# Cross attention with sparsemax and a nine-expert feed-forward: another order of the pipeline's pieces, one value product for both row tiles, and round signals and buffers doubled by parity

## The reference

```
q  = LN(x) @ Wq + bq;  k = ctx @ Wk + bk;  v = ctx @ Wv + bv      # 16 heads of 16
s  = (q . k) / 4                                                  # 256 x 16 heads x 77
a  = sparsemax(s)                                                 # max(s - tau, 0), tau so that it sums to 1
x1 = x + (a . v) @ Wo + bo
z  = LN(x1);  l = z @ gate_w.T
two experts of eight are chosen by l + lb_bias; their weights are sigmoid(l), divided by their sum
y  = x1 + sum over experts e of weight_e * (relu(z @ w1_e.T)^2 @ w2_e.T)
        + relu(z @ cfc.T)^2 @ cproj.T                             # the shared expert
```

## Time and profile before

| | |
|---|---|
| executions | 870.45, 864.1, 865.37 us; median 865.37 |
| span of the profiled execution | 863.6 us |
| PE busy | 768.4 us, 89% of the span |
| DVE busy | 606.6 us, 70% |
| POOL busy | 518.4 us, 60% |
| ACT busy | 461.1 us, 53% |
| DMA moved | 34.88 MB |

### The profile page before, as it was taken

The page is one execution under the profiler, slowest core; times in us unless marked ns, Lnnn a source line. Parts: engine busy times, 40 slices in busy tenths (PEclk is TensorE's granted clock), DMA queues, the critical chain, the costliest instruction groups (busy, mean ns, idle before and its releaser), DMA issues.

```text
span 863.6 us, 15088 instructions
## 1 busy us (share of the span) xinstructions
PE 768.4 (89%) x5056; PEld 628.9 (73%) x5056; DVE 606.6 (70%) x1827; ACT 461.1 (53%) x794; POOL 518.4 (60%) x590
## 2 busy tenths in 40 slices
PE   1666449999999899999999999999999999899998
PEld 1544337877878787878788787877787888688877
DVE  1788977878687878777786877887877778742221
ACT  1545454656655566656566566656665656442321
POOL 2459585758666675757586766667575757541010
PEclk9958668999999999999999999999999999999999
DMA  8300001020202002020102020110202020202010
GB/s 254 124 7 14 8 12 51 13 66 5 75 1 74 9 14 62 13 68 16 62 5 74 6 74 2 50 32 14 62 13 68 3 62 2 61 2 62 2 62 12
DMA packets 37358, 34.88 MB, mean 40 GB/s; under 512 B 23153, under 2 KB 34078, under 8 KB 35230
## 3 DMA queue, kind: packets, MB, share of 16 engines
q1 hardware_dynamic: 34934, 28.88, 11.9%
q0 software_dynamic: 1248, 4.73, 1.6%
q10 hardware_dynamic: 1096, 0.29, 0.2%
HBM read 28.30 MB, written 4.33 MB: 38 GB/s over the span
## 4 chain that ended last, share of the span: by engine, by line
PE 41%; DVE 23%; POOL 11%; DMA 11%; issue 8%; ACT 3%; DVEq 1%; ACTq 0%; POOLq 0%
PE y_ps L816 14%; PE h_ps L803 11%; DVE fsum L947 8%; DMA sw_all<-sw_scratch 8%; POOL over L342 7%; PE m_ps L767 6%; PE s_ps L759 4%; PE m_ps L776 4%; DVE g L1092 3%; DVE fold_a L959 2%; ACT hid L577 2%; DMA sw_scratch<-swT 2%; DVE den L967 1%; DVE f_stats L895 1%; DVE ln_stats L895 1%
## 5 line engine op out<-in xcount | busy, mean ns | idle before, releaser
L342 POOL TENSOR_TENSOR over<-S,tau 128x1232 f32<-128x1232 f32 x128 | 286.5, 2249 | 201.3 <-DVE tau L977 198.8
L816 PE MATMUL y_ps<-w_sb,hid 128*128 128x256 f32 x1152 | 279.1, 385 | 23.0 <-ACT hid L577 22.9
L803 PE MATMUL h_ps<-x1nT,w_sb 128*128 128x256 f32 x1152 | 275.6, 382 | 0.0
L816 PEld LDWEIGHTS y_ps<-w_sb,hid 128*128 128x128 f32 x1152 | 211.6, 190 | 65.5 <-ACT hid L577 37.5
L803 PEld LDWEIGHTS h_ps<-x1nT,w_sb 128*128 128x128 f32 x1152 | 215.1, 191 | 30.5 <-issue 2.8
L577 ACT ACTIVATE hid<-g 128x512 f32<-128x512 f32 x144 | 89.9, 625 | 113.3 <-DVE g L1092 112.8
L947 DVE TENSOR_REDUCE fsum<-over 128x16 f32<-128x1232 f32 x96 | 137.0, 1427 | 16.2 <-POOL over L342 13.8
L1092 DVE SCALAR_TENSOR_TENSOR g<-h_ps,sw_all 128x512 f32<-128x512 f32 x128 | 87.5, 684 | 75.1 <-PE h_ps L803 43.0
L526 ACT ACTIVATE signs<-over 128x1232 bf16<-128x1232 f32 x96 | 115.1, 1225 | 22.9 <-POOL over L342 22.9
L923 DVE MAX8 top<-S 128x8 f32<-128x77 f32 x512 | 74.6, 223 | 3.3 <-ACT S L516 3.3
L342 POOL TENSOR_TENSOR attn<-S,tau 128x1232 f32<-128x1232 f32 x32 | 71.8, 2263 | 6.1 <-PE s_ps L759 5.8
(11 more groups left out here) (111 smaller groups left out, 941.9 us busy)
## 6 DMA issues: line engine op xcount, KB each, us to landing
sw_all<-sw_scratch SPq DMA_DIRECT2D x16, 1024.0 KB, 5.3
x_sb<-in_x SPq DMA_DIRECT2D x16, 256.0 KB, 2.7
w_sb<-in_w POOLq DMA_DIRECT2D x2, 2048.0 KB, 12.0
out_y<-wk_sb SPq DMA_DIRECT2D x16, 256.0 KB, 5.7
sw_all<-in_ctx SPq DMA_DIRECT2D x1, 1078.0 KB
v_block<-v_all SPq DMA_DIRECT2D x56, 9.6 KB
wk_sb<-in_wk SPq DMA_DIRECT2D x1, 256.0 KB
wv_sb<-in_wv SPq DMA_DIRECT2D x1, 256.0 KB
```

Of the source, the lines that this page charges most:

```text
L342: return pool.tensor_tensor(dst, S[:, p, t, :, 0:NK], tau[:, p, t].rearrange("p (h o) -> p h o", o=1).broadcast_to([P, NH, NK]), ALU.subtract)
L803: last = pe.matmul(h_ps[:, i % 2, c, :], w1_sb[:, e, k, c * P:(c + 1) * P], x1nT[:, p, k, :], start=(k == 0), stop=(k == KC - 1))
L816: last = pe.matmul(y_ps[:, t, :], hid[:, i % 2, c, t * P:(t + 1) * P], w2_sb[:, e, c, :], start=(i == 0 and t == 0 and c == 0), stop=(i == ...
```

## The change

1. New order. `turns` now runs b = -1 to 18. The pieces are called one by one in a new order on every engine. The feed-forward part of batch f begins in turn f+2 (layer1 0 to 7, layer2 0 to 4) and ends in turn f+3 (layer2 5 to 8, layer1 8). The attention product of batch m is in PE's turn m+1 instead of m+2, and so are output, second norm and route. `newton` is cut into `round_sum`, `round_lean`, `round_fold`, `round_count`, `round_step`, `last_sum`, `last_step`. The count of unsettled rows moves from y_ps to a bank of s_ps.
2. Joint value product. `attnT` holds both tiles. Both tiles' attention is turned first, with layer1(4) between, then `late_heads` multiplies once: 17 blocks with 256 rows moving; one ACT copy of 512 numbers per partition to OT, then `late_output` for both tiles.
3. A signal for each load: eight semaphores in the place of `w_att`, each waited for where its data is used first. The feed-forward weights are issued by SP. The start values are raised half by POOL, half by PE.
4. Signals and small buffers of the rounds (`fold_a`, `fold_b`, `lean`, `fsum`, `rden`, `step`) are doubled by the batch's parity.

The core of the diff:

```diff
-        attnT = sb("attnT", [P, CHUNKS, P])
+        attnT = sb("attnT", [P, CHUNKS, TOK])
-        tau_first, tau_ready = sig("tau_first", T), sig("tau_ready", ROUNDS)
+        tau_first, tau_ready = sig2("tau_first", T), sig2("tau_ready", ROUNDS)
...
-            for b in range(NB + 3):
-                turn(b, b % 2, 1 - b % 2, new=b < NB, mid=1 <= b < NB + 1, late=2 <= b < NB + 2, old=b >= 3,
-                     ahead=b < NB - 1)
+            for b in range(-1, NB + 3):
+                turn(b, b % 2, 1 - b % 2, ahead=b < NB - 1, new=0 <= b < NB, mid=0 <= b - 1 < NB, late=0 <= b - 2 < NB,
+                     old=b >= 3)
...
-            for s in signals:
-                pool.sem_inc(s.sem, s.per)
+            for s in signals[0::2]:
+                pool.sem_inc(s.sem, s.per)
...
+            for s in signals[1::2]:
+                pe.sem_inc(s.sem, s.per)
             pe.wait_ge(consts, N_CONSTS)
+            pe.wait_ge(ident_loaded, 16)
...
+            def late_heads(m):
                 pe.wait_ge(v_placed[m // 2 % 2], 16 * len(PIECES) * (m // RING + 1))
+                pe.wait_ge(gate_chain.sem, gate_chain.at(m - 1, 1))
                 for i, blocks in enumerate(BY_BANK):
-                    pe.wait_ge(aT_taken.sem, aT_taken.at(m, SB * t + i + 1))
+                    pe.wait_ge(aT_taken.sem, aT_taken.at(m, SB + i + 1))
                     for c, a in blocks:
-                        last = pe.matmul(m_ps[32 * quad:32 * quad + 32, t, half * P:(half + 1) * P],
+                        last = pe.matmul(m_ps[32 * quad:32 * quad + 32, 0, half * TOK:(half + 1) * TOK],
                                          v_block[0:rows, m % RING, BLOCKS.index((c, a)), :], attnT[0:rows, c, :],
                                          start=c == order[0], stop=c == order[-1])
...
+            def late_heads(m):
+                act.wait_ge(o_done.sem, o_done.at(m))
                 act.wait_ge(wo_done.sem, wo_done.at(m - 1))
-                act.activation(OT[:, :, t * P:(t + 1) * P], pair(t), ACT.Copy).then_inc(o_taken.sem, 1)
+                act.activation(OT[:].rearrange("p k n -> p (k n)"), m_ps[:, 0, :], ACT.Copy).then_inc(o_taken.sem, 1)
...
-    nc = bacc.Bacc("TRN2", target_bir_lowering=False, num_devices=1)
+    nc = bacc.Bacc("TRN2", target_bir_lowering=False, num_devices=1, dynamic_dma_scratch_size=1024)
```

More of the change, by code:

```diff
@@ L83, in sig, with sig2 @@
             return signals[-1]
+        def sig2(name, per):
+            return [sig(f"{name}_{p}", per) for p in range(2)]
         def plain(name):
@@ L871, in turn @@
+                if b in (0, 1):
+                    pair_values(4 * b + 2)
+                if late:
+                    layer1(b - 2, p, 4)
+                if mid:
+                    late_pieces(b - 1, 1, 1)
+                    late_pieces(b - 1, 1, 2)
+                    late_heads(b - 1)
+                    late_output(b - 1, 0)
+                    late_output(b - 1, 1)
+                if b in (0, 1):
+                    pair_keys(4 * b + 2)
                 if late:
-                    late_turned(b - 2)
@@ new lines, in turn @@
+                if b in (0, 1):
+                    pair_keys(4 * b + 3)
+                if mid:
+                    late_turned(b - 1, 0)
+                    late_turned(b - 1, 1)
+                if b == -1:
+                    pair_keys(0)
+                if late:
+                    layer1(b - 2, p, 5)
+                if b == 0:
+                    pair_context(4)
+                if mid:
+                    late_route(b - 1, q)
+                if late:
+                    layer2(b - 2, 3)
@@ L883, in _ @@
+                if b == 0:
+                    pair_values(4)
+                if late:
+                    layer1(b - 2, p, 6)
+                    layer1(b - 2, p, 7)
+                    layer2(b - 2, 4)
             turns(pe, turn)
@@ L1161, in turn @@
+            def turn(b, p, q, ahead, new, mid, late, old):
+                if mid:
+                    round_sum(b - 1, q, 2, 0)
+                if old:
+                    old_gates(b - 3, q, 6)
+                if mid:
+                    round_fold(b - 1, q, 2, 0)
+                    round_sum(b - 1, q, 2, 1)
                 if late:
@@ L1163, in turn @@
                 if mid:
[L1164 to L1168 removed]
+                    round_fold(b - 1, q, 2, 1)
+                    round_count(b - 1, q, 2)
+                    round_step(b - 1, q, 2)
+                if old:
+                    old_gates(b - 3, q, 7)
+                    old_gates(b - 3, q, 8)
+                if ahead:
+                    new_stats(b + 1, q)
@@ L1171 @@
+                if late:
+                    old_gates(b - 2, p, 4)
+                    old_gates(b - 2, p, 5)
+                if new:
+                    round_lean(b, p, 2)
+                if b in (0, 1):
+                    pair_values(4 * b + 3)
+                if mid:
+                    late_gate(b - 1)
+            turns(dve, turn)
 def kernel(**inputs):
```

716 lines of the change are left out of this document (383 added, 333 removed).

## The result

The changed kernel took 842.1, 844.06, 845.25 and 838.47 us, median 843.08; the kernel before, run beside it, took 870.45, 864.1, 865.37 and 865.09, median 865.23. The ratio is 0.9721, with a 95% interval of 0.9675 to 0.9767: 22 us faster, inside the predicted range of 807 to 850 and 18 us above the forecast of 825. The profiled execution took 842.1 us and its span is 840.3, so the 1.8 us between span and time, which the sum had added, hold here too.

The account below looks back on a forecast made before the run. Early turns were taken as bound by the chain of threshold rounds, steady turns by PE's own work. Span 863.6 less 32.5 (start) less 8 (turns) is 823, plus 1.8 gives 825 us; range 807 to 850.

Parts of the forecast that it names:

- From there to the first layer1: Chain from round 1 of batch 0 to the first layer1, now in turn 2: 98 us against 132.0, bounds 90 and 108.
- pairs of keys and values: Early turns: these pairs stand in all four queues before the first layer1; 2 us added for them.
- The rest of PE's work behind it is the same as before, so the gain at the start is 32.5.: After the first layer1: 34 us earlier less 1.5 us for batch 2's scores leaves 32.5, if turns keep their length.
- The turns count 15 times: Steady turns over the whole run: 0.55 us saved in each of 15 turns, 8 us together.
- The steady turn: Distance of two late_roots: set by two loops of 46.1 and 45.2 us, taken as 46.4 against 46.98.
- mixed loop: From the tau ending round 1 through POOL's subtractions and shares, PE to late_output(1), then DVE's residual, statistics and round 1: 45.2 us.
- Today's waits are covered.: DVE's gate on the spread shares, 1.9 us: the spread lands about 16 us after the tau, DVE arrives 24 us after.
- A: Rival on the steady turn: it shrinks more, to 45.3 us, giving 809 us; chance 0.14.
- B: Rival: early layer1 comes, but PE waits for OT's copy and banks behind ACT's signs; turn 48 us, time 849; chance 0.11.
- D: Rival in ACT's queue: copies wait behind a sign for POOL's late subtraction; turn 49.8, time 875 us, slower; chance 0.05.
- C: Rival at the start: chain of rounds in turns 0 and 1 unchanged, first layer1 at 112, time 839 us; chance 0.08.
- E: Rival: the change does nothing since PE is full anyway, near 865 us; chance 0.02, shared with anything else near no change.

## Why the prediction was right, and where it missed

The direction and the main mechanism were right: the first layer1 comes a turn earlier. The second part of the forecast, shorter turns, brought nothing in sum, and the time stayed inside the range since the range was wide enough for it. By its steps:

**PE's start.** Predicted 5, measured 6.86 (bounds 4 and 11.3). First root predicted 7, measured 6.24; first scores predicted 14, measured 14.56; round 1 of batch 0 predicted 31.5, measured 31.60. The run with the start undone gives its worth in the new order, 9 us of the time; alone, in the old order, it brought 7.

**From there to the first layer1.** Predicted 98, measured 105.9: 7.9 us late, within the bounds of 90 to 108. POOL's timeline dates the slip:

```profile
49.37 4.46 POOL L347 TENSOR_TENSOR over<-S,tau 128x1232 f32<-128x1232 f32 x2 [4.39 <-DVE tau L1043]
59.68 2.26 POOL L347 TENSOR_TENSOR attn<-S,tau 128x1232 f32<-128x1232 f32 x1 [4.90 <-DVE tau L1054]
...
91.02 4.49 POOL L347 TENSOR_TENSOR over<-S,tau 128x1232 f32<-128x1232 f32 x2 [4.39 <-DVE tau L1043]
```

Up to 49 the walk was right within half a microsecond. Round 3 was to end at 56.5 and ends at 59.7: ACT's relus stand behind the copy of batch 1's turned tile, which PE makes only after a pair of keys (51.92 above). Round 0 of batch 1 was to end at 74 and ends at 78.9, two more lost. Its round 1 was to end at 83 and ends at 90.9, another three. DVE's timeline shows why:

```profile
82.10 0.42 DVE L1132 TENSOR_TENSOR x<-m_ps,xb 128x256 f32<-128x256 f32 x1 [1.98 <-PE m_ps L824]
...
84.81 1.43 DVE L1007 TENSOR_REDUCE fsum<-over 128x16 f32<-128x1232 f32 x1
```

POOL's first subtraction of that round was through at 81.3, but DVE first waits for batch 0's output and does its residual and statistics, and sums only from 84.81. The subtractions of round 2, which were to end at 87.5, begin at 91.0 and end at 95.5; late_roots, predicted at 92 before the addition for pairs, is at 100.0. The queries then take 3.78 us, since PE had waited 7.58 before them, and with the transposes 5.9 us lie between late_roots and the first layer1 where the walk had 4. So the chain was 10 us longer than walked, against which the prediction had only the 2 us for "pairs of keys and values". That term was mis-sized: moving a single pair gave back 1.6 us, and DVE's residual and statistics, about 2.7 us ahead of round 1, had no term at all.

**"The rest of PE's work behind it is the same as before, so the gain at the start is 32.5."** This is the step that failed most. Earlier by 132.0 - 105.9 = 26.1 us, the first layer1 brought only 23.3 us of span (863.6 - 840.3), although the steady turn also became shorter. From the first layer1 to the end it takes 734.4 us; before, it took 731.6. The work is the same, its place isn't. In turn 2 the feed-forward part of the batch before doesn't exist, so the turn holds 14 groups of eight instructions; groups of PE by line between 105.8 and 148.0, where L850 and L862 have 64 + 48 = 112 instructions:

```profile
L850 PE MATMUL h_ps<-x1nT,w_sb 128*128 128x256 f32 x64 | 17.2, 420 | 0.3 <-DVE g L1174 0.3
L862 PE MATMUL y_ps<-w_sb,hid 128*128 128x256 f32 x48 | 11.1, 381 | 0.0
```

A full turn has 18. Yet turn 2 lasts 48.04 us: PE waits 3.46 us for DVE's verdict, and the next eight instructions run at half clock, 3.41 us:

```profile
117.12 0.24 PE L780 MATMUL s_ps<-ones,unsettled 128*1 128x1 f32 x4 [3.46 <-DVE below L1079]
117.72 3.41 PE L850 MATMUL h_ps<-x1nT,w_sb 128*128 128x256 f32 x8 [0.26 <-DVE g L1174]
```

The four missing groups come at the end. After the last late_roots the kernel before has 74 + 72 = 146 such instructions and the change 98 + 80 = 178, 32 more, four groups; this tail is 840.3 - 798.6 = 41.7 us where it was 36.5. Groups of PE by line behind the last late_roots, in the kernel before:

```profile
L816 PE MATMUL y_ps<-w_sb,hid 128*128 128x256 f32 x74 | 17.5, 380 | 1.4 <-ACT hid L577 1.4
L803 PE MATMUL h_ps<-x1nT,w_sb 128*128 128x256 f32 x72 | 16.8, 379 | 0.0
```

And in the change:

```profile
L862 PE MATMUL y_ps<-w_sb,hid 128*128 128x256 f32 x98 | 22.3, 379 | 0.0
L850 PE MATMUL h_ps<-x1nT,w_sb 128*128 128x256 f32 x80 | 18.2, 379 | 0.0
```

**"The turns count 15 times".** Neither did this hold. In the eleven turns that the 46.98 comes from, the gain was right in kind, 0.40 us each and not 0.55. But the old order's last three turns were already 45.45, 43.87 and 42.02 us; two of them lie behind the last batch's stage new. In the new order the feed-forward parts begin a turn earlier, and only one such turn is left, of 44.90. From the first late_roots to the last the fifteen turns took 827.07 - 131.62 = 695.4 us before and take 798.57 - 100.00 = 698.6 now: 3.1 more, and not 8 less.

**The miss in numbers.** 7.9 us by the later first layer1. Behind it 734.4 were measured and 823 - 98 = 725 predicted, 9.4 more. The turns are 11 us worse than forecast: 8 of it in the last three, the rest in turn 2 and in the smaller gain of the others. The two ends give about 2 back. The tail is 5.2 longer, but the first layer1 stands 5.9 us behind its late_roots where it was 0.4, which takes 5.5 out of the stretch behind it, and the prediction had added 1.5 there. Together 17.3 us, 840.3 - 823 of span.

**The steady turn.** Predicted 46.4, measured 46.59. The wait on the bare copy was predicted at 0.7 and is 0.70; the 0.3 for the bank behind a sign doesn't show ahead of the product. The product was predicted at 2.6 and takes 2.38; split it takes 2.41, so its gain is nothing, the lower bound. The Trainium skill holds against many small matmuls that each has an overhead of about 60 cycles ("TensorEngine Tiling (Array Packing)", Instruction Overhead); here, in four column groups, half the instructions save 0.03 us. By the PSUM Bottleneck section of that page of the Trainium skill the copy out of PSUM may become the bottleneck. The trace agrees: PE's wait of 0.70 us for the bare copy is what the joint product brought.

"Both being close, they will disturb each other" was right in the sum and wrong in the ranking. The forecast had PE's own loop as the longer one (46.1 against 45.2). The run with layer2 between product and output shows that the mixed loop binds, and the split kernel with x first shows its length without the copy: 45.68. The walk without its 0.7 for the copy has 44.5, so it was 1.2 us short: it counted PE as working straight on from late_roots to the output, and in the chain above PE's layer1(3) and layer1(4) stand behind DVE's eight largest, verdict and gate, with 0.9 us of waits. PE's own work was put at 45.15 us a turn and is 44.4, so the loop that was named first was too long by 0.7. The closeness of 46.4 to 46.59 is therefore partly luck, two errors that cancel. And the copy costs what it does not because PE idles but because output, residual and round 1 come later.

**"Today's waits are covered."** Right for the shares: no gate waits for them. But SP's queue was walked for the spread only, and not for the load of x that stands beside it behind the same 21 us. It is late in five turns (10.7 us in the waits above, the longest 2.6). It costs nothing while the product is joint (844.56 us without that wait), and much once it is split (839.51 against 828.54).

**Parity costs nothing.** Right, and it brings nothing.

**Rivals.** A (turn 45.3) didn't come, but it is close to what the split product with x first gives, 45.68. B and D didn't come: no wait in microseconds stands ahead of the product. C was partly right, the first layer1 slipped by half of what it said. E, no change, didn't come.

**What brought the 22 us.** The start, 7 us alone and 9 in the new order. The doubling, nothing measurable. The joint product, a loss of about 3.6 us as it stands, which isn't clear of noise, and of 16 once x is early. The new order is the rest: 22.2 - 9.0 + 3.6 = some 17 us by this sum, and 21 by the two runs that differ by it (860.39 and 839.51). Its first layer1 is a turn earlier in the chain, and it has no waits of layer2 for squares (22.9 us before) and of gates for the shares (31.1 us of DVE's before); what each of these is worth was not separated.

## What to carry to other kernels

When a pipeline starts earlier, count the work of the first turn in the new order: what can't be done there comes back in the tail, and a first turn that is set by a chain doesn't get shorter with less work. And count the last turns of the old order as they are, since a pipeline that runs empty has shorter ones, and an earlier start takes these away. Fewer and larger matmuls gained nothing here, where four column groups already ran side by side, while a copy left bare costs by whatever loop runs through it, so ask first which loop that is: put a piece of work over the bare wait, and see if the time falls or rises. Walk every load behind a long row of small DMAs, not just the one that waited before; two limits that lie level hide each other, and the gain of some 15 us here appeared only with both moved.

## What the runs showed of the hardware

After a wait inside a full stream the next eight matmuls may run at half clock, 1.2 GHz instead of 2.4: 3.41 us after 3.46 of wait, 3.22 after 2.35 in the kernel with the start alone, and 3.67 us in turn 16, where PE had waited 2.23, in place of 1.99. Over these 3.7 us in turn 16 the granted clock was 0.54; in the steady stretch above it was 1.00. In PE's timeline of the change, turn 16:

```profile
768.37 0.24 PE L780 MATMUL s_ps<-ones,unsettled 128*1 128x1 f32 x4 [2.23 <-DVE below L1079]
769.01 3.67 PE L850 MATMUL h_ps<-x1nT,w_sb 128*128 128x256 f32 x8 [0.30 <-DVE g L1174]
```

But the length of the wait doesn't decide it. In the kernel before, a group behind a longer wait runs at full clock:

```profile
290.70 1.99 PE L816 MATMUL y_ps<-w_sb,hid 128*128 128x256 f32 x8 [2.73 <-ACT hid L577]
```

In the kernel with the pair of keys moved, the wait of 2.22 us in turn 16 is followed by 1.99 us too, and with the power left out five of eight waits of 1.6 us were followed by half clock and three were not. So such a wait can cost up to 1.8 us more than itself, and whether it does was not to be foreseen from these runs.

A shorter operation in the binding loop gave no gain: with the power left out another loop of about the same length seems to have taken over, and with the half clock behind its waits the time was 832.3 instead of 828.5 us.
